# Scan stage of a two-layer kernel: the product with B two steps ahead of the scan, in three buffers

## What is computed

```python
dt = softplus(einsum('blr,cr->blc', dbl[..., :DT_RANK], W_dt) + b_dt)
Bs = dbl[..., DT_RANK:DT_RANK + D_STATE]
Cs = dbl[..., DT_RANK + D_STATE:]
A = -exp(A_log)
def step(h, inp):
    dt_t, B_t, C_t, u_t = inp
    dA = exp(dt_t[:, :, None] * A)
    h = h * dA + (dt_t * u_t)[:, :, None] * B_t[:, None, :]
    y = einsum('bcs,bs->bc', h, C_t)
    return (h, y)
_, ys = scan(step, h0, xs)
y = swapaxes(ys, 0, 1) + u * D_skip
y = y * silu(z)
```

## Time and profile before

| | us |
|---|---|
| median of 3 runs | 2197.11 |
| lowest, highest | 2188.95, 2199.14 |
| profiled execution, its own time | 2187.27 |
| its span in the trace | 2185.5 |
| VectorE busy | 1669.4 |
| TensorE busy | 1866.1 |
| ScalarE busy | 1263.6 |
| GpSimd busy | 1214.6 |

### The profile page before, as it was taken

One profiled execution on the slowest core, in us unless ns is written; L12 is line 12 of the kernel. 1 busy time (PEld: TensorE's weight loads), 2 busy tenths in 40 slices (PEclk: granted clock), 3 DMA queues, 4 the chain that ended last, 5 costly groups with the idle time before them and its releaser, 6 DMA issues. The chain is left out here.

```text
span 2185.5 us, 26582 instructions
## 1 busy us (share of the span) xinstructions
PE 1866.1 (85%) x8596; PEld 1058.5 (48%) x8596; DVE 1669.4 (76%) x2189; ACT 1263.6 (58%) x1685; POOL 1214.6 (56%) x651
## 2 busy tenths in 40 slices
PE   6689988997998898789879888998886677998996
PEld 3345545654654463233334332533342235887885
DVE  4975797397579525899999999999989995332787
ACT  4764874586486515666654665466544434655774
POOL 2601810360181002789988999888976674222676
PEclk9899999999999999899999999999988999999998
DMA  7420641344064216899898888988899984223453
GB/s 203 97 59 6 148 99 58 106 95 109 15 140 97 78 35 44 288 312 286 280 319 300 285 286 295 306 290 275 296 298 368 331 327 140 97 96 101 140 160 105
DMA packets 177321, 402.68 MB, mean 184 GB/s; under 512 B 48174, under 2 KB 77104, under 8 KB 176034
## 3 DMA queue, kind: packets, MB, share of 16 engines
q1 hardware_dynamic: 165154, 371.09, 54.9%
q0 software_dynamic: 12032, 29.90, 4.8%
HBM read 356.30 MB, written 45.51 MB: 184 GB/s over the span
## 5 line engine op out<-in xcount | busy, mean ns | idle before, releaser
L1336 POOL TENSOR_TENSOR late<-late,rows 128x1024 f32<-128x1024 f32 x256 | 602.5, 2361 | 144.8 <-DVE late L1816 141.6
L1987 PE MATMUL m_Q<-late,ident_m 128*128 128x512 f32 x1024 | 524.4, 644 | 152.8 <-POOL late L1336 119.3
L1816 DVE TENSOR_TENSOR_SCAN late<-m_Q,late 128x1024 f32<-128x1024 f32 x256 | 586.2, 2290 | 44.9 <-ACT m_Q L1522 16.4
L1522 ACT ACTIVATE m_Q<-late,acol 128x1024 f32<-128x1024 f32 x256 | 286.1, 1118 | 368.4 <-DVE late L1816 366.7
L1987 PEld LDWEIGHTS m_Q<-late,ident_m 128*128 128x128 f32 x1024 | 193.7, 201 | 449.6 <-POOL late L1336 253.2
L1809 DVE TENSOR_TENSOR late<-m_Q,rows 128x1024 f32<-128x1024 f32 x256 | 306.9, 1199 | 9.9 <-DMA rows<-bc_s 9.8
L553 DVE SCALAR_TENSOR_TENSOR early<-early,work 128x1024 f32<-128x1024 f32 x128 | 155.9, 1218 | 43.7 <-ACT early L699 41.7
L2050 PE MATMUL m_Q<-late 128*128 128x128 f32 x1248 | 158.8, 281 | 9.0 <-issue 1.3
L2050 PEld LDWEIGHTS m_Q<-late 128*128 128x128 f32 x1248 | 147.0, 193 | 36.3 <-issue 35.0
L709 ACT ACTIVATE early<-early 128x1024 f32<-128x1024 f32 x128 | 135.2, 1056 | 26.9 <-DVE early L558 25.8
L710 ACT ACTIVATE early<-early,halfpi 128x1024 f32<-128x1024 f32 x128 | 145.7, 1138 | 0.0
(11 more groups left out here) (243 smaller groups left out, 3340.9 us busy)
## 6 DMA issues: line engine op xcount, KB each, us to landing
rows<-bc_s SPq DMA_DIRECT2D x512, 512.0 KB, 5.7
rows<-st_s SPq DMA_DIRECT2D x64, 384.0 KB, 5.8
r_s<-late SPq DMA_DIRECT2D x39, 256.0 KB, 2.0
rows<-st_s SPq DMA_DIRECT2D x64, 128.0 KB, 6.4
st_s<-early SPq DMA_DIRECT2D x8, 768.0 KB, 5.3
xin<-in_x SPq DMA_DIRECT2D x4, 1024.0 KB, 5.6
xres<-in_x SPq DMA_DIRECT2D x4, 1024.0 KB, 5.5
mx_s<-s SPq DMA_DIRECT2D x4, 1024.0 KB, 4.5
```

The source lines that it names most:

```text
L1336: nc.gpsimd.tensor_tensor(pr[:, n % NH, :], h[:, n % NH, :], cb[:, n % NCB, :], ALU.mult).then_inc(pr_ok, 1)
L1522: A(dA[:, :], dt[:, (b * KI + m) % 2, :], ACT.Exp, scale=acol[:, m, i % NS:i % NS + 1]).then_inc(dA_ok, 1)
L1816: v_.tensor_tensor_scan(h[:, n % NH, :], dA[:, :], dB[:, n % 2, :], 0.0, ALU.mult, ALU.add).then_inc(h_ok, 1)
L1987: ins = mm(half(Y, c), ident[:, :], half(pr[:, n % NH, :], c), start=False, stop=(n % NS == NS - 1), skip_group_check=True)
```

## The change

`dB` gets a third buffer (`ND` = 3), and `late` grows by one tile to hold it. VectorE makes products 0 and 1 ahead of scan 0 and then, behind scan n, product n + 2. The product of step n waits for scan n - 3, whose buffer it takes. ScalarE's `drive_out` moves from behind the decay of step 15 of a block to behind the decay of step 14; it waits for the same two things as before. Buffers of B, C, h and pr stay as they are, and so do the lists of SP, GpSimd and TensorE.

```diff
-NBB, NCB, NH, NU = 3, 4, 3, KI + 1
+NBB, NCB, NH, NU, ND = 3, 4, 3, KI + 1, 3
...
-        late = sb("late", [P, 10 * L])
+        late = sb("late", [P, 11 * L])
...
-        dB = part(late, 6 * L, [2, L])
-        dt = part(late, 8 * L, [2, L])
+        dB = part(late, 6 * L, [ND, L])
+        dt = part(late, (6 + ND) * L, [2, L])
...
-        first = part(late, 8 * L, [2, 2 * D])
+        first = part(late, (6 + ND) * L, [2, 2 * D])
...
-                        if s == NS - 1 and b * KI + m + 1 < B * KI:
+                        if s == NS - 2 and b * KI + m + 1 < B * KI:
                             drive_out(b * KI + m + 1)
...
-                    if n >= 2:
-                        dv.wait_ge(h_ok, n - 1)
-                    v_.tensor_tensor(dB[:, n % 2, :], du[:, :], bb[:, n % NBB, :], ALU.mult).then_inc(dB_ok, 1)
+                    if n >= ND:
+                        dv.wait_ge(h_ok, n - ND + 1)
+                    v_.tensor_tensor(dB[:, n % ND, :], du[:, :], bb[:, n % NBB, :], ALU.mult).then_inc(dB_ok, 1)
...
-                    v_.tensor_tensor_scan(h[:, n % NH, :], dA[:, :], dB[:, n % 2, :], 0.0, ALU.mult, ALU.add).then_inc(h_ok, 1)
+                    v_.tensor_tensor_scan(h[:, n % NH, :], dA[:, :], dB[:, n % ND, :], 0.0, ALU.mult, ALU.add).then_inc(h_ok, 1)
...
                 times_b(0)
+                times_b(1)
                 for n in range(B * STEPS):
                     scan(n)
-                    if n + 1 < B * STEPS:
-                        times_b(n + 1)
+                    if n + 2 < B * STEPS:
+                        times_b(n + 2)
```

## The result

The changed kernel is slower: 2237.51 us (median of 4 runs, 2233.80 to 2242.75) against 2198.12 us (median of 4, 2188.95 to 2199.41; the table of before has the first three of them), ratio 1.0189 with a 95% interval of 1.016 to 1.0219. Its profiled execution took 2236.89 us, 49.6 us more than that of before.

The account below looks back on a forecast made before the run. ScalarE's decay behind each scan was taken to set the quiet step, so nothing is saved; 15.4 + 16.6 + 12.6 + 2.6 + 6.0 - 5.4 = 47.8 us on 2197.11 gives 2245 us, range 2208 to 2278.

Parts of the forecast that it names:

- Bound: Quiet step, 3.53 us: the decay behind the scan decides, by 0.04 us over VectorE's own path; saving there 0.
- Rows of B: Loads of B wanted one step, 3.54 us, sooner than SP's queue brings them: terms of 15.4, 16.6 and 12.6 us.
- held in SP's queue: Steps 12 and 201, three stores and an expert load, where SP's queue holds B's load: 16.6 us together.
- Behind GpSimd: Steps where B's load stands behind a load of C waiting for GpSimd's late product: 15.4 us lost.
- Crowded: Fourteen places between 40 and 249 where B falls short, landings taking 6.6 us in the median: 12.6 us together.
- Start: Scan 0 stands behind a second product, 1.2 us, and its B may land up to 1.4 late: 2.6 us.
- The copy: Blocks 2 and 3 of a batch: ScalarE's sooner copy waits for dus; four of seven blocks count, 6.0 us.
- Given back: VectorE's 16.4 us of waits for a late ScalarE, a third regained while B holds VectorE: 5.4 us.
- (a): Only held places, start and copy count, as loads leaving in pairs land faster: +20 us, 2217 us; chance 12%.
- (b): In crowded stretches the queue sets landings, so leaving sooner brings nothing: +25 us, 2270 us; chance 20%.
- (c): VectorE's own 0.13 us hand-over, not the decay, holds the scan: 0.21 us a step, 2195 with other terms; 4%.
- (d): GpSimd's lag disappears as waits for B bring it level; only steps 12, 201 and start cost: +9, 2206; 6%.

Follow-up runs that it names:

- half-decay kernels: Decay makes only 512 of 1024 columns from step 1 on: in the kernel before, ratio 0.9955; in the changed kernel with B's load first and dus sooner, 0.983.

## Why the prediction was right, point by point

The forecast was 2245 us in a range of 2208 to 2278, with the sum at +47.8 us; measured were 2237.51 us, +39.4 in the medians and +43.8 in the stage of the profiles. The signs named came as named: step 12 waits 6.55 us, B is waited for 52.9 us in 35 places, the copy seven times.

- **Bound.** The quiet step stayed at 3.54 us with the scan 0.03 us behind the decay, as said. That the decay decides, and not VectorE's equal path, was read off the gaps; the half-decay kernels show it, and the 0.04 us between the two paths came out as 3.54 to 3.50.
- **Rows of B.** Forecast +44.6 us and 1.4 at the start; measured 52.9 - 9.8 = +43.1. By kind: held in SP's queue (12, 61, 125, 189, 197, 201, 203) 22.5 us in the changed kernel, 8.0 before: 14.5 for 16.6. Behind GpSimd (32 to 34, 50, 67, 78, 79, 97, 98, 115, 142, 143, 160) 11.6 for 15.4. Crowded (eleven stretches from 39 to 249) 15.8 for 12.6: the last was under-sized; the largest places outside the last batch are 85 and 149, whose loads left right behind the store of the output (L1237) and took 9.8 and 10.2 us to land. One reading behind these terms was off: a landing was taken as 5.1 us in a quiet stretch and some 5.4 behind GpSimd, but leaving 0.36 us behind C it was 6.3. That the terms came out near all the same, with GpSimd standing 184.0 us for VectorE instead of 141.6 and so behind less often, is in part luck. Step 61 lost 1.5 us, not 3.5 with its neighbour, and 197 lost 2.7, not 1.0: sums held, single places did not.
- **Start.** 2.6 forecast. The first scan starts 3.68 us behind the first product's start (888.12, 884.44) instead of 1.33: 2.35.
- **The copy.** The mechanism and its size a block were right (1.33 to 1.38 us in five blocks, 2.55 and 2.59 in two), but the term was 11.9 us in seven blocks, not 6.0 in four. The step that failed is "three lie where VectorE already waits for B": a wait there holds up GpSimd's product of step 12 as well, so dus moves along with it and the copy waits as long as elsewhere. The kernel with B's load first bears this out: its waits for B at 61, 125 and 189 are gone, and the copy's there are the same, 1.33, 2.57 and 1.35 us. There is a shadow of another kind: with the copy's wait taken away, waits for B and for the decay grew, and only 3.6 us of stage were won.
- **Given back.** 5.4 us forecast; the idle time ahead of the scan fell by 11.3, 6.9 of it waits for ScalarE; most of the rest is the 0.13 us between product and scan, which is gone in 37 steps whose product came late and was not needed by that scan. The too small copy term and this one nearly cancel, which is luck: 46.0 + 1.2 + 6.0 - 5.4 = 47.8 forecast; 43.1 + 11.9 - 11.3 = 43.7 by the measured idle times. The second product at the start is in this sum at the other end: the last scan has no product in front of it and VectorE waits 1.24 us for its decay. In the medians the change is 39.4 us; that this is 4 us less than in the stage is not explained.
- **Rivals.** (a), loads in pairs landing faster, is refuted: with nearly all loads in pairs the median landing of both rows is 5.9 us over the span, it was 5.7, and the second of a pair, which is B, lands later than before. (b), the full queue: the kernel with B's load first refutes it as the main cause, 43 of 53 us went with the order of issue alone. (c), the decay not binding: refuted by both half-decay kernels. The 0.13 us that it took for VectorE's own hand-over is time in which the scan waits for the decay: where the decay was out of the way, the scan followed the product it waited for by 0.09 us, in 227 of 256 steps. (d), GpSimd's lag vanishing: it fell, but 11.6 us were left.

## What to carry to other kernels

Equal sums on two paths are a warning: before an operation is moved ahead, look at which hand-over gap stays constant: here it was the path that set the step, and the other's gain was nothing. Making a consumer run one step further ahead moves the deadline of everything it reads; if the buffers and the order of the loads stay, the room shrinks by a step, and a load that stands in one queue behind another's wait lost it first here. Issue the load with the earliest deadline first; here that alone gave back 1.8 of 1.9%.

## What the runs showed of the hardware

A VectorE operation that follows one it need not wait for started 0.08 to 0.09 us before that one's recorded end; one that waited for it, 0.09 to 0.10 us after it. One such hand-over a step, from product to scan, is nearly all of the difference between 3.31 and 3.50 us. Half an activation of 1024 columns, 512, took 0.66 to 0.69 us in the place of 1.12, not half. Of two 512 KB loads issued less than 0.6 us apart in one queue the second landed later: 6.3 us in the median against 5.3 for the first in the changed kernel (B behind C, some 230 pairs), and 6.2 against 5.2 in the kernel before with the order turned round (C behind B, some 200 pairs). And one operand of VectorE's product moved from PSUM to SBUF turned 1.20 us into 2.28 us on average beside a GpSimd that is busy 81% of the stage.
